# States scanned into SBUF, the last one kept by ScalarE, decays in four PSUM banks two steps ahead, four product buffers

## The chip, the core and the metric

The program runs on one core of a Trainium2 chip. The metric is the device time of one execution in microseconds (us). The core's engines run side by side and meet at semaphores: TensorE (PE, with its weight loads PEld) for matrix products, VectorE (DVE), ScalarE (ACT) and GpSimd (POOL) for elementwise work, SyncE (SP) for most transfers. SBUF is the working memory of 128 partitions, PSUM holds what TensorE writes, in 8 banks of 512 f32 elements a partition. GpSimd works on SBUF here.

## What is computed

4096 tokens (2 sequences of 2048) of width 256 pass through a mixture of experts with half weight, a Mamba block with an MLP behind it, and the same mixture of experts again. The change lies in the middle part. Cut to what matters, for each of 512 inner channels e and 16 states s:

```python
dA = jnp.exp(dt_t[..., None] * A)                       # decay
h = h * dA + (dt_t * u_t)[..., None] * B_t[:, None, :]  # state, a recurrence over the tokens t
y = jnp.einsum('bes,bs->be', h, C_t)                    # sum over the 16 states
...
y = tm(ys) + x_conv * D
y = y * silu(z)
return jnp.einsum('bte,de->btd', y, out_proj_w)
```

Behind it: `x = x + mamba(...)`, an rms norm, `square(relu(fc))` and a projection back to 256.

## The kernel before, in words

The middle part (`mamba`) takes the tokens in 8 chunks of 512 (CT), which lie in the free dimension; the 512 inner channels are 4 groups of 128 partitions, taken as 2 pairs p. For a chunk k (a "turn") there are 32 steps n = p*16 + s, one for each pair and state. A step does, for the two groups j of its pair:

- ScalarE, `decay`: dA = exp(A*DT) into PSUM bank B_DA + j (banks 2 and 3), one step ahead. It waits until the scan of the step before has read that bank (`scanned`).
- GpSimd, L1291: dB = DTU * B (one instruction of 128x1024, both operands in SBUF), into one of two buffers. It waits for the scans of two steps before, and so runs up to two steps ahead.
- VectorE, L1397: `tensor_tensor_scan`, h = dA*h + dB over 512 tokens, from PSUM (dA) and SBUF (dB) into PSUM bank B_H + j (banks 4 and 5). Its start value is a column of the state table ST.
- VectorE, L1406 (`weigh`): G = h * C, PSUM and SBUF in, SBUF out, two buffers; between the two weighs of a step L1413 copies the last column of both states into ST, with a bit mask that sets them to zero at the end of a sequence (`kept`).
- TensorE, L1101: transposes G and adds it into the sum over the states (banks 6 and 7).
- SP: loads the rows of B and C of the step, spread over the partitions, 4 buffers (L972).

Every engine runs its program in the order written. Besides the steps there is the work of the next chunk's front (norm, input product, convolution, dt) and of the chunk before's back (`out` product, norm, MLP). Tables (LATE, EARLY, BACK) say at which step n of a turn an engine does which item: the four numbers are the steps on PE, ACT, DVE and POOL. Those that matter here: on ScalarE `silu` at 19 (two table loads and two activations of 128x2048), `sq` at 9; on VectorE `out` at 5 and 7, `v` at 10 (L1378, the 128x4 sums of squares times 1/D plus eps), `pj` at 30 and 31; on GpSimd `add` (L1266, DT) at 6 and 27, `du` (L1270, DTU) at 7 and 28, `v` (L1276, the power -1/2) at 12, `xa` (L1280) at 14 and 16. Items stand behind the step's own work. At steps 0 and 16 VectorE does `gated` (L1365, 128x1024, PSUM and SBUF in) between the scans and the weighs.

In the mixture of experts two lines are spoken of below: L302 (VectorE, a product of two SBUF tensors of 320 elements) and L341 (GpSimd, a difference of two SBUF tensors of 320 elements), and L261, a short scan from SBUF to SBUF.

## Time and profile before

| | |
|---|---|
| time, median of 3 runs | 2183.04 us (2175.22 to 2190.57) |
| time of the profiled execution | 2182.28 us |
| its span (first to last instruction) | 2180.4 us |
| the scan stage in it | 591.8 to 1607 us |
| busy over the span | PE 1725.6, DVE 1709.5, POOL 1242.9, ACT 977.6 us |

The profile has one line for each instruction on each engine with its start and duration. A group of the costliest instructions is a line of the kernel with an engine and its shapes; behind it stand how often it ran, its busy time, its mean in ns, the idle time of the engine ahead of it and what ended that idle time ("<-DVE PS L1397" is: until VectorE's L1397 was done). In a timeline an instruction that has a release stands with it in square brackets. Instructions of one engine overlap by some tens of ns, so a chain of them is counted from start to start.

### The profile page before, as it was taken

The numbers are of one execution on the slowest core, as the hardware profiler recorded it, in microseconds if no ns is written. First come the engines' busy times: TensorE is split into PE (matmuls) and PEld (weight loads), VectorE is DVE, ScalarE is ACT, GpSimd is POOL, SyncE is SP. The second block draws the span as 40 slices with busy tenths as digits, with TensorE's granted clock in tenths as the row PEclk, the third lists the DMA queues.
The fourth block names the chain that finished last, engine by engine and source line by source line (L and its number), as shares of the span: only waits on it lengthen the run. The fifth ranks groups of instructions, "written<-read, shape, count | busy, mean of one in ns | idle before, by whom it ended". The sixth has DMA issues, their size and how long they took to land. (4 is left out here: it accounts for less than half of the span.)

```text
span 2180.4 us, 35658 instructions
## 1 busy us (share of the span) xinstructions
PE 1725.6 (79%) x10728; PEld 1411.5 (65%) x10729; DVE 1709.5 (78%) x2990; ACT 977.6 (45%) x1507; POOL 1242.9 (57%) x751
## 2 busy tenths in 40 slices
PE   5279999993886878879787787877577379999996
PEld 5279999993344546545464554545456269999996
DVE  4857666665498999989999999989955757766665
ACT  2333333331465566566666656665431323333331
POOL 1257455555476767767676676767631246545555
PEclk8589999997877898989999898988686579999998
DMA  6244343343343434434344443443412334333342
GB/s 193 79 120 105 69 86 82 82 70 90 121 137 126 140 127 141 136 122 143 127 136 127 137 136 127 136 128 136 142 36 97 97 102 106 81 74 87 82 78 26
DMA packets 161018, 237.96 MB, mean 109 GB/s; under 512 B 29370, under 2 KB 85296, under 8 KB 160304
## 3 DMA queue, kind: packets, MB, share of 16 engines
q1 hardware_dynamic: 130096, 198.84, 28.7%
q0 software_dynamic: 30720, 36.53, 10.1%
q8 instruction: 115, 1.88, 0.4%
q14 instruction: 87, 0.71, 0.1%
HBM read 202.57 MB, written 38.34 MB: 110 GB/s over the span
## 5 line engine op out<-in xcount | busy, mean ns | idle before, releaser
L1291 POOL TENSOR_TENSOR m_dB<-m_DTU,m_BC 128x1024 f32<-128x1024 f32 x256 | 604.0, 2362 | 308.0 <-DVE PS L1397 307.5
L1397 DVE TENSOR_TENSOR_SCAN PS<-PS,m_ST,m_dB 128x512 f32<-128x512 f32 x512 | 628.3, 1271 | 58.7 <-POOL m_dB L1291 27.1
L1110 ACT ACTIVATE PS<-m_DT,m_A 128x512 f32<-128x512 f32 x512 | 351.1, 690 | 361.3 <-DVE PS L1397 360.1
L1101 PEld LDWEIGHTS PS<-keep_ident,m_G 128*128 128x128 f32 x2048 | 254.9, 153 | 207.8 <-DVE m_G L1406 168.2
L1101 PE MATMUL PS<-keep_ident,m_G 128*128 128x128 f32 x2048 | 313.5, 297 | 90.2 <-DVE m_G L1406 89.7
L1406 DVE TENSOR_TENSOR m_G<-PS,m_BC 128x512 f32<-128x512 f32 x512 | 340.8, 673 | 10.3 <-PE PS L1101 10.2
L603 PE MATMUL PS<-e_xh,e_wh 128*128 128x256 f32 x1008 | 295.0, 293 | 0.5 <-DVEq L491 0.2
L603 PE MATMUL PS<-e_xl,e_wh 128*128 128x256 f32 x1008 | 289.0, 287 | 0.0
L603 PE MATMUL PS<-e_xh,e_wl 128*128 128x256 f32 x1008 | 288.8, 287 | 0.0
L660 ACT ACTIVATE e_hh<-e_u 128x512 fp32r<-128x512 f32 x252 | 157.9, 633 | 281.1 <-DVE e_u L716 280.9
L621 PE MATMUL PS<-e_wh,e_hh 128*128 128x256 f32 x1008 | 281.4, 279 | 0.0
L621 PE MATMUL PS<-e_wl,e_hh 128*128 128x256 f32 x1008 | 280.5, 278 | 0.0
L621 PE MATMUL PS<-e_wh,e_hl 128*128 128x256 f32 x1008 | 280.1, 278 | 0.0
L528 POOL DMA_INDIRECT e_xin<-xrows,e_gix x160 | 199.8, 1249 | 57.5 <-issue 43.1
L534 POOL DMA_INDIRECT out<-e_ysb,e_six x80 | 134.5, 1682 | 157.4 <-DVE e_ysb L740 136.7
L534 POOL DMA_INDIRECT sums<-e_ysb,e_six x80 | 136.8, 1710 | 150.4 <-DVE e_ysb L740 133.1
L735 DVE TENSOR_TENSOR e_ysb<-PS,e_b 128x512 f32<-128x512 f32 x80 | 55.2, 690 | 189.6 <-PE PS L621 184.0
L603 PEld LDWEIGHTS PS<-e_xh,e_wh 128*128 128x128 f32 x1008 | 198.6, 197 | 1.2 <-DVEq L491 0.8
L603 PEld LDWEIGHTS PS<-e_xl,e_wh 128*128 128x128 f32 x1008 | 198.8, 197 | 0.0
L603 PEld LDWEIGHTS PS<-e_xh,e_wl 128*128 128x128 f32 x1008 | 197.6, 196 | 0.0
L716 DVE TENSOR_TENSOR e_u<-PS,keep_b 128x512 f32<-128x512 f32 x252 | 170.0, 687 | 27.0 <-PE PS L603 16.1
L621 PEld LDWEIGHTS PS<-e_wl,e_hh 128*128 128x128 f32 x1008 | 189.3, 188 | 0.0
(200 smaller groups left out, 2908.1 us busy)
## 6 DMA issues: line engine op xcount, KB each, us to landing
m_BC<-bc_rows SPq DMA_DIRECT2D x512, 256.0 KB, 3.3
layer_raw<-w SPq DMA_DIRECT2D x64, 512.0 KB, 3.9
xrows<-r_xn SPq DMA_DIRECT2D x16, 512.0 KB, 4.2
keep_X<-x SPq DMA_DIRECT2D x4, 1024.0 KB, 9.6
sums<-keep_X SPq DMA_DIRECT2D x4, 1024.0 KB, 11.1
out<-keep_X SPq DMA_DIRECT2D x4, 1024.0 KB, 11.0
keep_X<-sums SPq DMA_DIRECT2D x3, 1024.0 KB, 13.4
e_xin<-xrows,e_gix POOLq DMA_INDIRECT x160, 3.3
```

What stands on the lines that cost most here:

```text
L528: G.indirect_dma_start(out=xin[:, c % CPE, t, :], out_offset=None, in_=xrows, in_offset=column(gix, c, t), bounds_check=last_token, oob_is ...
L534: G.indirect_dma_start(out=sums, out_offset=column(six, c, t), in_=ysb[:, c % CPE, t, :], in_offset=None, compute_op=ALU.add, bounds_check ...
L603: last = M(PS[:, B_S1 + pair, m * CH:(m + 1) * CH], a, r, start=(n == 0), stop=(n == len(terms) - 1))
L621: last = M(PS[:, B_Y + c % 2, t * D:(t + 1) * D], a, r, start=(n == 0), stop=(n == len(terms) - 1))
L660: A(hh[:, c % 2, 2 * pair:2 * pair + 2, :], u[:, pair, :, :], ACT.Relu).then_inc(hh_ok, 1)
L716: V.tensor_tensor(u[:, pair, :, :], PS[:, B_S1 + pair, :].rearrange("p (m c) -> p m c", m=2), b1.unsqueeze(2).to_broadcast([P, 2, CH]), AL ...
L735: V.tensor_tensor(ysb[:, c % CPE, :, :], PS[:, B_Y + c % 2, :].rearrange("p (t d) -> p t d", t=CHT), b2.unsqueeze(1).to_broadcast([P, CHT, ...
L1101: last = M(PS[:, B_Y + j, ts], G[:, s % 2, j, ts], C["ident"][:, :], is_transpose=True, start=False, stop=(s == DS - 1 and a == CTT - 1))
L1110: return nc.scalar.activation(out, in_, func, **kw)
L1291: G_.tensor_tensor(dB[:, s % 2, :, :], DTU[:, es, :], BC[:, s % NBC, 0:1, :].to_broadcast([P, 2, CT]), ALU.mult).then_inc(dB_ok, 1)
L1397: V.tensor_tensor_scan(PS[:, B_H + j, :], PS[:, B_DA + j, :], dB[:, s % 2, j, :], ST[:, s, e:e + 1], ALU.mult, ALU.add).then_inc(scanned, 1)
L1406: V.tensor_tensor(G[:, s % 2, j, :], PS[:, B_H + j, :], BC[:, s % NBC, 1, :], ALU.mult).then_inc(g_ok, 1)
```

## The change

- Scans write an SBUF buffer HS (two steps deep) and not PSUM; the weighs read it there.
- The two banks that the states had go to the decays: four banks, two steps ahead (`AHEAD`).
- G has four buffers in place of two.
- The last column of the states is copied into ST by ScalarE (`keep`: an ACTIVATE Copy with a scale of 1 or 0 from `fmask`), after the decays of the step, and VectorE's L1413 with its mask goes.
- `v`: ScalarE's Square takes the factor 1/sqrt(D); GpSimd adds eps just ahead of the power, and VectorE's L1378 goes. The item moves from GpSimd's step 12 to 11.
- To make room T3 and HID share one tensor TH of six parts, and hT is xrT.

The diff, without its imports and with the repeats of a pattern left out:

```diff
-        T3 = sb("T3", [P, EK, CT])
-        HID = sb("HID", [P, EK, CT])
+        TH = sb("TH", [P, 6, CT])
+        T3 = TH[:, 0:EK, :]
+        def hid(e, n=1):
+            at = e + 4 if e < 2 else e
+            return TH[:, at:at + n, :]
-        hT = sb("hT", [P, DK, CT])
+        hT = xrT
-        G = sb("G", [P, 2, 2, CT])
+        NG, NH = 4, 2
+        G = sb("G", [P, NG, 2, CT])
+        HS = sb("HS", [P, NH, 2, CT])
-        B_DA, B_H, B_Y = 2, 4, 6
+        B_DA, B_Y, AHEAD = 2, 6, 2
...
-("v", 0): (_, _, 10, 12),
+("v", 0): (_, _, _, 11),
...
@@ TensorE
-                                last = M(PS[:, B_Y + j, ts], G[:, s % 2, j, ts], C["ident"][:, :], is_transpose=True,
+                                last = M(PS[:, B_Y + j, ts], G[:, n % NG, j, ts], C["ident"][:, :], is_transpose=True,
@@ ScalarE
-                        last = F(XR[:, t, :], XP[:, t, :], ACT.Square, accum_out=ssq[:, t:t + 1])
+                        last = F(XR[:, t, :], XP[:, t, :], ACT.Square, scale=1.0 / math.isqrt(D), accum_out=ssq[:, t:t + 1])
...
-                    if not (is_first(k) and n == 0):
-                        act.wait_ge(scanned, k * (2 * STEPS) + (2 * (n - 1) + j + 1))
-                    F(PS[:, B_DA + j, :], DT[:, e, :], ACT.Exp, scale=A[:, e, s:s + 1]).then_inc(dA_ok, 1)
+                    if not (is_first(k) and n < AHEAD):
+                        act.wait_ge(scanned, k * (2 * STEPS) + (2 * (n - AHEAD) + j + 1))
+                    F(PS[:, B_DA + 2 * (n % AHEAD) + j, :], DT[:, e, :], ACT.Exp, scale=A[:, e, s:s + 1]).then_inc(dA_ok, 1)
+            def keep(k, p, s):
+                n = p * DS + s
+                F(ST[:, s, 2 * p:2 * p + 2], HS[:, n % NH, :, CT - 1], ACT.Copy, scale=fmask[:, bass.ds(k + 1, 1)]).then_inc(kept, 1)
...
-                        if n + 1 < STEPS:
-                            decay(k, (n + 1) // DS, (n + 1) % DS)
+                        if n + AHEAD < STEPS:
+                            decay(k, (n + AHEAD) // DS, (n + AHEAD) % DS)
                         elif has_front:
-                            decay(k + 1, 0, 0)
+                            decay(k + 1, 0, n + AHEAD - STEPS)
+                        if n + AHEAD < STEPS or has_front:
+                            keep(k, p, s)
@@ GpSimd
                 if kind == "v":
+                    gp.wait_ge(sq_ok, k + 1)
+                    G_.tensor_tensor(ssq[:, :], ssq[:, :], eps[:, :], ALU.add).then_inc(v_ok, 1)
                     gp.wait_ge(v_ok, k + 1)
                     G_.tensor_tensor(ssq[:, :], ssq[:, :], mhalf[:, 0, 0:CTT], ALU.pow).then_inc(rs_ok, 1)
@@ VectorE
-                elif kind == "v":
-                    dve.wait_ge(sq_ok, k + 1)
-                    V.tensor_scalar(ssq[:, :], ssq[:, :], 1.0 / D, RMS_EPS, ALU.mult, ALU.add).then_inc(v_ok, 1)
...
-                            if not (is_first(k) and n == 0):
-                                dve.wait_ge(g_ok, k * (2 * STEPS) + (2 * n + j - 1))
-                                dve.wait_ge(kept, k * STEPS + n)
+                            if not (is_first(k) and n < NH):
+                                dve.wait_ge(g_ok, k * (2 * STEPS) + (2 * (n - NH) + j + 1))
+                                dve.wait_ge(kept, k * STEPS + (n - NH + 1))
...
-                            V.tensor_tensor_scan(PS[:, B_H + j, :], PS[:, B_DA + j, :], dB[:, s % 2, j, :], ST[:, s, e:e + 1],
+                            V.tensor_tensor_scan(HS[:, n % NH, j, :], PS[:, B_DA + 2 * (n % AHEAD) + j, :], dB[:, s % 2, j, :], ST[:, s, e:e + 1],
...
-                            V.tensor_tensor(G[:, s % 2, j, :], PS[:, B_H + j, :], BC[:, s % NBC, 1, :], ALU.mult).then_inc(g_ok, 1)
+                            V.tensor_tensor(G[:, n % NG, j, :], HS[:, n % NH, j, :], BC[:, s % NBC, 1, :], ALU.mult).then_inc(g_ok, 1)
...
-                        if not (is_first(k) and n < 2):
-                            dve.wait_ge(g_read, k * STEPS + (n - 1))
+                        if not (is_first(k) and n < NG):
+                            dve.wait_ge(g_read, k * STEPS + (n - NG + 1))
                         weigh(0)
-                        dve.wait_ge(scanned, k * (2 * STEPS) + (2 * n + 2))
-                        V.tensor_tensor(ST[:, s, 2 * p:2 * p + 2].bitcast(U32), PS[:, B_H:B_H + 2, CT - 1].bitcast(U32),
-                                        mask[:, bass.ds(k + 1, 1)].to_broadcast([P, 2]), ALU.bitwise_and).then_inc(kept, 1)
                         weigh(1)
```

## Rows read from the trace of the kernel before

**Rows 1.** The page's first part: busy us (share of the span) xinstructions.

```profile
PE 1725.6 (79%) x10728; PEld 1411.5 (65%) x10729; DVE 1709.5 (78%) x2990; ACT 977.6 (45%) x1507; POOL 1242.9 (57%) x751
```

**Rows 2.** Windows: the scan stage; length, busy (x) of PE, PEld, DVE, ACT, POOL.

```profile
591.80:1607.00 1015.20, 800.11 (x3634) 528.72 (x3635) 970.68 (x1329) 621.46 (x973) 694.58 (x306) 0.87 0.41 132
```

**Rows 3.** Groups of the scan stage, shapes kept apart: busy, mean ns, idle before.

```profile
L1397 DVE TENSOR_TENSOR_SCAN PS<-PS,m_ST,m_dB 128x512 f32<-128x512 f32 x512 | 628.3, 1271 | 58.7 <-POOL m_dB L1291 27.1 <-ACT PS L1110 26.6 <-issue 4.2
L1406 DVE TENSOR_TENSOR m_G<-PS,m_BC 128x512 f32<-128x512 f32 x512 | 340.8, 673 | 10.3 <-PE PS L1101 10.2
L1413 DVE TENSOR_TENSOR m_ST<-PS,m_mask 128x2 uint32<-128x2 uint32 x256 | 36.3, 142 | 0.0
...
L1270 POOL TENSOR_TENSOR m_DTU<-m_DT,m_U 128x1024 f32<-128x1024 f32 x15 | 35.4, 2360 | 0.0
L1266 POOL TENSOR_TENSOR m_DT<-m_DT,m_sp 128x1024 f32<-128x1024 f32 x15 | 35.4, 2358 | 5.8 <-ACT m_sp L1110 5.8
L1280 POOL TENSOR_TENSOR keep_X<-keep_X,m_XP 128x512 f32 x12 | 15.3, 1277 | 0.0
L1276 POOL TENSOR_TENSOR m_ssq<-m_ssq,m_mhalf 128x4 f32<-128x4 f32 x7 | 7.1, 1018 | 0.7
```

**Rows 4.** Timeline: start, duration us; VectorE through steps 18 to 21, POOL once.

```profile
1047.85 2.45 DVE L1397 TENSOR_TENSOR_SCAN PS<-PS,m_ST,m_dB 128x512 f32<-128x512 f32 x2
1050.21 0.66 DVE L1406 TENSOR_TENSOR m_G<-PS,m_BC 128x512 f32<-128x512 f32 x1
1050.81 0.14 DVE L1413 TENSOR_TENSOR m_ST<-PS,m_mask 128x2 uint32<-128x2 uint32 x1
1050.87 0.67 DVE L1406 TENSOR_TENSOR m_G<-PS,m_BC 128x512 f32<-128x512 f32 x1
1051.47 2.45 DVE L1397 TENSOR_TENSOR_SCAN PS<-PS,m_ST,m_dB 128x512 f32<-128x512 f32 x2
...
1058.74 2.47 DVE L1397 TENSOR_TENSOR_SCAN PS<-PS,m_ST,m_dB 128x512 f32<-128x512 f32 x2 [3.58 <-ACT PS L1110]
...
1050.38 2.36 POOL L1291 TENSOR_TENSOR m_dB<-m_DTU,m_BC 128x1024 f32<-128x1024 f32 x1 [1.25 <-DVE PS L1397]
```

**Rows 5.** Timeline, ScalarE: decays around the silu block, and a small scaled copy.

```profile
1050.33 0.69 ACT L1110 ACTIVATE PS<-m_DT,m_A 128x512 f32<-128x512 f32 x1 [0.48 <-DVE PS L1397]
...
1057.93 1.30 ACT L1110 ACTIVATE PS<-m_DT,m_A 128x512 f32<-128x512 f32 x2
...
1001.47 0.29 ACT L1110 ACTIVATE m_XI<-m_XI,m_fmask 128x12 f32<-128x12 f32 x1
```

**Rows 6.** Line L1378 (ns min/median/max), and the timeline around one of them.

```profile
L1378 DVE TENSOR_SCALAR m_ssq<-m_ssq x8: 170/1305/1362, 760.7 to 1623.1; 128x4 f32<-128x4 f32 x8
...
1015.48 2.36 POOL L1291 TENSOR_TENSOR m_dB<-m_DTU,m_BC 128x1024 f32<-128x1024 f32 x1 [1.25 <-DVE PS L1397]
...
1016.57 1.30 DVE L1378 TENSOR_SCALAR m_ssq<-m_ssq 128x4 f32<-128x4 f32 x1
1017.78 2.46 DVE L1397 TENSOR_TENSOR_SCAN PS<-PS,m_ST,m_dB 128x512 f32<-128x512 f32 x2
```

**Rows 7.** First experts layer: timeline of L302 and L341, and the line L341.

```profile
86.62 0.88 DVE L302 TENSOR_TENSOR r_inblock<-r_hot,r_tile_no 128x320 bf16<-128x320 f32 x2
86.89 1.19 POOL L341 TENSOR_TENSOR r_hot<-r_count,r_high 128x320 f32<-128x320 f32 x1 [2.34 <-PE PS L409]
...
87.03 0.48 DVE L302 TENSOR_TENSOR r_inblock<-r_hot,r_tile_no 128x320 bf16<-128x320 f32 x1
...
L341 POOL TENSOR_TENSOR r_hot<-r_count,r_high x32: 713/721/1203, 79.1 to 1737.0; 128x320 f32<-128x320 f32 x32
```

**Rows 8.** Timeline of a step 16: gated on VectorE, dB on POOL.

```profile
1038.23 1.20 DVE L1365 TENSOR_TENSOR m_YT<-PS,m_SZ 128x1024 f32<-128x1024 f32 x1
...
1038.40 2.36 POOL L1291 TENSOR_TENSOR m_dB<-m_DTU,m_BC 128x1024 f32<-128x1024 f32 x1 [1.26 <-DVE PS L1397]
```

**Rows 9.** Timeline: the scans from SBUF to SBUF, 32 elements each.

```profile
69.10 2.10 DVE L261 TENSOR_TENSOR_SCAN r_inc<-r_zcol,r_tot 128x32 f32<-128x32 f32 x16
```

More of the change, by code:

```diff
@@ L1 @@
+import math
 import concourse.bass as bass
@@ L782, in mamba @@
         taps = sb("taps", [P, EK, DC, P])
-        mask = sb("mask", [P, MCH + 1], U32)
-        fmask = sb("fmask", [P, MCH])
+        fmask = sb("fmask", [P, MCH + 1])
         st = sb("st", [P, 2 * CTT, 6])
@@ L789, in mamba @@
         mhalf = sb("mhalf", [P, 2, 2 * CTT])
+        eps = sb("eps", [P, CTT])
         XI = sb("XI", [P, EK, DC - 1 + CT])
         U = sb("U", [P, 2, EK, CT])
-        T3 = sb("T3", [P, EK, CT])
-        HID = sb("HID", [P, EK, CT])
+        TH = sb("TH", [P, 6, CT])
[3 more added lines that the diff above has]
+            return TH[:, at:at + n, :]
         xrT = sb("xrT", [P, DK, CT])
-        hT = sb("hT", [P, DK, CT])
+        hT = xrT
         XR = sb("XR", [P, CTT, D])
@@ L848, in mamba @@
             ("g", 2): (1, 2, _, _), ("g", 3): (2, 3, _, _),
-            ("out", 0): (4, _, 5, _), ("out", 1): (6, _, 7, _), ("sq", 0): (_, 9, _, _), ("v", 0): (_, _, 10, 12),
+            ("out", 0): (4, _, 5, _), ("out", 1): (6, _, 7, _), ("sq", 0): (_, 9, _, _), ("v", 0): (_, _, _, 11),
             ("hr", 0): (_, 13, _, _), ("hT", 0): (19, 20, _, _), ("hT", 1): (21, 22, _, _), ("xa", 0): (_, _, _, 14), ("xa", 1): (_, _, _, 16),
@@ L1061, in back @@
                 elif kind in ("out", "pj"):
-                    at, src = (W_OUT, T3) if kind == "out" else (W_PJ, HID)
+                    at, src = (W_OUT, lambda e: T3[:, e:e + 1, :]) if kind == "out" else (W_PJ, hid)
                     if kind == "out":
@@ L1069, in back @@
                         for e in range(EK):
-                            last = M(bank(p, k)[:, (t % 2) * D:(t % 2 + 1) * D], src[:, e, t * P:(t + 1) * P],
+                            last = M(bank(p, k)[:, (t % 2) * D:(t % 2 + 1) * D], src(e)[:, 0, t * P:(t + 1) * P],
                                      weights(at, D, e, 0, D), start=(e == 0), stop=(e == EK - 1))
@@ L1208, in back @@
                     wait_written(act, p, k)
-                    F(HID[:, n, :], bank(p, k), ACT.Relu).then_inc(read(p, k), 1)
+                    F(hid(n)[:, 0, :], bank(p, k), ACT.Relu).then_inc(read(p, k), 1)
                 elif kind == "q":
                     wait_read(act, k, ("fc", 2 * n), ("fc", 2 * n + 1))
-                    F(HID[:, 2 * n:2 * n + 2, :], HID[:, 2 * n:2 * n + 2, :], ACT.Square).then_inc(q_ok, 1)
+                    F(hid(2 * n, 2), hid(2 * n, 2), ACT.Square).then_inc(q_ok, 1)
             def decay(k, p, s):
@@ L1222, in decay @@
                     e, n = 2 * p + j, p * DS + s
-                    if not (is_first(k) and n == 0):
-                        act.wait_ge(scanned, k * (2 * STEPS) + (2 * (n - 1) + j + 1))
-                    F(PS[:, B_DA + j, :], DT[:, e, :], ACT.Exp, scale=A[:, e, s:s + 1]).then_inc(dA_ok, 1)
+                    if not (is_first(k) and n < AHEAD):
[4 more added lines that the diff above has]
+                F(ST[:, s, 2 * p:2 * p + 2], HS[:, n % NH, :, CT - 1], ACT.Copy, scale=fmask[:, bass.ds(k + 1, 1)]).then_inc(kept, 1)
             def turn(k, par, has_front, has_back):
                 if is_first(k):
-                    decay(k, 0, 0)
+                    for s in range(AHEAD):
+                        decay(k, 0, s)
                 for p in range(PAIRS):
@@ L1301, in _ @@
             V.memset(mhalf[:, :, :], -0.5)
-            V.memset(fmask[:, :], 1.0)
-            link(V.memset(mask[:, :].bitcast(mybir.dt.int32), -1))
+            V.memset(eps[:, :], RMS_EPS)
+            link(V.memset(fmask[:, :], 1.0))
             V.memset(ST[:, :, :], 0.0)
@@ L1306, in _ @@
             for k in range(0, MCH, MCH // BATCH):
-                V.memset(fmask[:, k:k + 1], 0.0)
-                link(V.memset(mask[:, k:k + 1].bitcast(mybir.dt.int32), 0))
+                link(V.memset(fmask[:, k:k + 1], 0.0))
             def tile(k, t, n=1):
```

## The prediction

> **What bounds the kernel now.** I read the totals first [rows 1]. Over the whole span VectorE (DVE) and TensorE are both near 79% busy, which is an average over three stages. The diff touches one of them, the scan stage, so I cut it out: from the first scan at 591.8 us to 1607 us it lasts 1015 us, VectorE is busy for 971 of them, GpSimd (POOL) for 695 and ScalarE for 621 [rows 2]. VectorE sets the time there. Then the groups of that stretch [rows 3]: 512 scans, 512 products ("weigh", L1406) and 256 tiny state copies (L1413) make nearly all of VectorE's work. Its waits inside the stretch are small: 26.6 us for ScalarE's decays ahead of scans and 10.3 us for TensorE ahead of products; the 27.1 us put down to POOL are the wait before the very first scan.
>
> Next the timeline of one plain step [rows 4]: weigh at 1050.21, state copy at 1050.81, weigh at 1050.87, scans from 1051.47. Neighbours overlap a little, so I count start to start: 0.60 + 0.06 + 0.60 and 2.36 for the two scans, 3.62 us for a step. 256 steps of 3.62 are 927 us. POOL makes the next-but-one dB in 2.36 us of each step, starting 0.17 us after the first weigh, and sleeps 1.25 us. So POOL has slack today, and its work runs *at the same time* as the two weighs. That is legal today at no cost, because a weigh reads one operand from PSUM and one from SBUF. After the change it reads both from SBUF, and that is where my forecast turns.
>
> **The gains, part by part.**
>
> (a) State copy off VectorE: 0.06 to 0.07 us a step by the starts [rows 4], 256 steps: 17 us. The 142 ns of its row [rows 3] are mostly overlap. Its work goes to ScalarE; the nearest row is a small ACTIVATE with a pointer scale, 0.29 us [rows 5]. 256 of these are 75 us of an engine that idles for some 390 of 1015 us [rows 2]; it lies behind the decays and is needed only two steps later, so I cost it at nothing except in (c).
>
> (b) The tensor_scalar of L1378 leaves VectorE. It takes 170 ns with POOL idle and 1305 otherwise [rows 6]: seven times inside the stretch the next scan begins 1.21 us after it. 8.5 us.
>
> (c) Decays two steps ahead. At step 19 ScalarE runs a copy, two table loads and two silus between the decay at 1050.33 and the next at 1057.93 [rows 5], and VectorE stands 3.58 us [rows 4]. Afterwards scan 22 is the first to lack its decay. It is due three pairs of weighs and two pairs of scans after scan 19, 8.3 us by today's scans and 8.05 by those of (e). ScalarE is 0.7 us in the last decay, 0.3 in the copy, 6.9 in the block, then 1.25 in two decays and 0.25 in the copy that the scan now waits for: 9.3. About 1.2 us stay of 3.6. Seven turns and a shorter wait of the first chunk: 18 us gained. What is queued behind is then late by the keep as well: VectorE's scan waits for keep of two steps before, which stands in front of the block, so no new wait.
>
> (d) Four product buffers: weighs no longer wait for the transposes, 10 us of 10.3 [rows 3].
>
> (e) Scans write SBUF. No scan of 512 into SBUF is in the trace. Two points: start to start 1.18 for 512 into PSUM [rows 4], and 16 SBUF scans of 32 elements in 2.10 us [rows 9], so (2.10-0.21)/15 = 0.126. If the price is only elements, the slope is 2.2 ns and nothing is gained. If the fixed part is that of the other VectorE operations, about 0.06 us beside 1.04 ns an element (0.60 for 512 [rows 4], 0.40 for 320 [rows 7]), the short scan gives 2.1 ns an element, a long one 1.12, and the 0.06 left over belong to PSUM as destination. The bounds are 0 and 31 us; the common fixed part fits the more rows, so I take 31. A loss I exclude: VectorE already writes G to SBUF beside POOL at full rate [rows 4].
>
> (f) Weigh from two SBUF operands: 0 to +0.015 us each, I take +5 us in all. The weigh from PSUM (0.60 for 512) and the all-SBUF product (0.40 for 320) lie on one line of 1 ns an element.
>
> Sum of gains: 17 + 8.5 + 18 + 10 + 31 - 5 = 80 us. Buffers shared by T3/HID and xrT/hT cost nothing: their readers are done half a chunk before the next writer.
>
> The Trainium skill, VectorE: DVE Perf Modes, section on the TRN2 errata, gives 58 cycles beside the elements for SBUF to SBUF and 120 for PSUM to SBUF. It would shorten each weigh by 65 ns, 33 us in all; the line through the weigh and the all-SBUF product speaks against it.
>
> **The price: a door that both engines use.** L302 on VectorE multiplies two SBUF tensors, L341 on POOL reads two. A POOL L341 that starts 0.27 us into a pair of L302 takes 1.19 us in place of 0.72 (median 721, four such cases near 1200) and ends 0.72 after 87.37, that is when the *second* L302 has read its input [rows 7]. So POOL stands while VectorE reads two SBUF operands, and it isn't let in between two such products that follow closely. The other way round, L1378 ran until POOL's dB was over: end 1017.87 beside 1017.84 [rows 6]; the engine that waits gets in about 0.15 us before the recorded end of the other. That is a one-source operation; whether a two-source one is held likewise no row shows. I take it that it is.
>
> The Trainium skill, SBUF — State Buffer, section Who interferes with whom, says so: a Vector instruction with two SBUF inputs contends with a GpSimd instruction that reads SBUF, and who comes second is held for the whole instruction. For L341 the trace agrees (1194 to 1203 ns beside 721).
>
> Now a plain step after, with 0 at the first weigh: weighs at 0 and 0.60, door free at 1.13, dB runs 1.13 to 3.49, VectorE could enter from 3.35. Scans start at 1.20 and 2.32, next weigh at 3.43 (3.55 if (e) fails). It just fits: a plain step costs nothing. But POOL's slack is gone, and dB is only two buffers deep, so nothing is caught up. Every other visit to the door lands on VectorE:
> - `add` and `du`, 2.36 us each [rows 3], 30 in the stretch (two a chunk of either, less the two made before it). They begin as dB ends, hold the door to 5.80, the weigh enters at 5.65: 2.1 us each, 63. (If the weigh comes first by a hair, the next dB is late and the scan waits 2.3 instead.) Seven of them lie behind a VectorE `out`, 0.6 less each: 59.
> - `xa`, 1.27 us: 14 times 1.0, 14 us. `v`: its add of eps and the pow of 1.02 us, which waits behind the weighs and pushes dB: 7 times 0.8, 6 us.
> - At `gated` (steps 0 and 16) VectorE does a product from PSUM for 1.12 us first [rows 8], POOL's dB takes the door 0.17 us in and keeps it to 2.4: 1.25 us, 15 times, 19 us.
>
> Price 98 us. Net +18. The sum is made on the profiled execution (span 2180.4, time 2182.3, 0.8 below the median of the three runs); 2183 + 18.5 = 2202.
>
> **Rivals.**
> 1. The door is contended, but scans gain nothing from SBUF (e = 0; (c) gains 2 more): 2202 + 31 - 2 = 2231. For it: one slope of 2.2 also fits. 0.22.
> 2. The door costs nothing for f32 products beside dB, because a two-source read is not held by a running POOL instruction and dB isn't pushed past its due time. Then only gains are left: 2183 - 80 = 2103, or 2133 without (e). Its place is the weigh at 3.43; it decides from the point where add, du, xa and gated cost under 2.6 us a chunk in place of 12. For it: no row shows a held two-source product. Against it: L341. 0.13. A half-way form, in which only POOL is held and the 1.2 us between dB's end and the scan that needs it hide part of each visit (30 x 1.2 and the 19 of gated): 2202 - 55 = 2147, 0.06.
> 3. Weighs from SBUF also lose 0.06 us each: 2202 - 31 = 2171. Only the page on VectorE speaks for it (it says 65 ns). 0.08.
> 4. POOL gets in between the two weighs of a step. Then the second begins at 2.75, a step lasts 5.7 in place of 3.43: 256 x 2.27 = 581 more, less the 98, 2685. Against it: L302's pair held together with POOL waiting since 0.27; for it: there is a semaphore wait between the weighs. 0.06.
> 5. ScalarE's extra copies or anything else: 0.03.
>
> **How the numbers follow.** My forecast has 0.42, about 2188 to 2216. A measurement here can tell about 1% from no change, 22 us: 2161 to 2205. Rival 2 and its half-way form lie below: 0.20 with a little of 5. Rival 3 and somewhat over half of the forecast lie within: 0.35. The rest of the forecast, rivals 1 and 4 lie above: 0.45. For 8 in 10 the range must hold the forecast, 1, 3 and the half-way form, and a margin: 2125 to 2245.
>
> **What the profile after would show.** Right: weighs of some 0.68 us in plain steps and a second form of about 2.8 us (once for each add and du) or 1.9 (gated); dB of 2.36 in place but recorded as some 3.3 us, since it starts as before and waits; POOL busy near 900 us in the stretch; no idle before weighs by TensorE; ScalarE's wait near 1.2 us a chunk; scan starts 1.12 apart. Wrong: dB stays at 2.36 with weighs running beside it (rival 2); scans still 1.18 apart (rival 1); every second weigh near 2.9 (rival 4). A plain step longer than 3.6 us would say that the fit of dB between the weighs fails, and that I mis-sized the handing over of the door.

## The result, and the profile after

The changed kernel takes **2643.62 us** (median of 4 runs, 2641.18 to 2647.44) beside 2184.43 for the kernel before (4 runs on the same chip). The ratio is 1.2118, 95% interval 1.2088 to 1.2148. The forecast was 2202 with a range of 2125 to 2245; the time lies nearest to rival 4 (2685), which had a chance of 0.06.

The page's first part and the windows of the scan stage, after (columns as in [rows 1, 2]):

```profile
PE 1870.9 (71%) x10726; PEld 1472.0 (56%) x10729; DVE 2215.3 (84%) x2724; ACT 1032.2 (39%) x1761; POOL 1339.9 (51%) x759
...
591.40:2068.00 1476.60, 947.64 (x3634) 592.17 (x3634) 1476.55 (x1065) 674.87 (x1225) 793.43 (x313) 0.78 0.28 91
```

The whole loss lies in the stage that the change touches. It lasted 1015 us [rows 2] and lasts 1477; outside it both executions spend 1165 us. VectorE has 264 instructions fewer there and is busy for all of it, 1476.55 of 1476.60 us. The granted TensorE clock fell with TensorE's share of the time (0.87 to 0.78 in the stage), but no wait of VectorE for TensorE is left, so it sets nothing.

The groups of the stage, after (line, engine, operation, tiles, shapes, count; busy, mean ns; idle before), and then what the line of the weighs says (ns minimum, median, maximum):

```profile
L1423 DVE TENSOR_TENSOR m_G<-m_HS,m_BC 128x512 f32<-128x512 f32 x511 | 856.8, 1714 | 0.0
L1414 DVE TENSOR_TENSOR_SCAN m_HS<-PS,m_ST,m_dB 128x512 f32<-128x512 f32 x512 | 626.0, 1261 | 26.1 <-POOL m_dB L1312 26.1
...
L1312 POOL TENSOR_TENSOR m_dB<-m_DTU,m_BC 128x1024 f32<-128x1024 f32 x255 | 681.5, 2672 | 669.5 <-DVE m_HS L1414 669.5
L1289 POOL TENSOR_TENSOR m_DTU<-m_DT,m_U 128x1024 f32<-128x1024 f32 x15 | 42.0, 2797 | 0.0
...
L1121 ACT ACTIVATE m_ST<-m_HS,m_fmask 128x2 f32<-128x2 f32 x254 | 71.4, 281 | 0.0
...
L1423 DVE TENSOR_TENSOR m_G<-m_HS,m_BC x512: 655/679/2855, 593.8 to 2068.0; 128x512 f32<-128x512 f32 x171
```

Scans are what they were (1261 ns beside 1271 in [rows 3]). The weighs went from a mean of 673 to 1714 ns, but not evenly: the median is 679, the maximum 2855. That is two kinds, one weigh untouched and one very long. VectorE's idle time is nothing except the wait before the first scan. A kernel that has lost 460 us shows *no waits* on the engine that sets its time: the loss stands inside the duration of an instruction, and only the gap between median and mean gives it away.

The timeline of one step, after (start, duration us; VectorE, then GpSimd):

```profile
1171.06 3.42 DVE L1423 TENSOR_TENSOR m_G<-m_HS,m_BC 128x512 f32<-128x512 f32 x2
1174.40 2.44 DVE L1414 TENSOR_TENSOR_SCAN m_HS<-PS,m_ST,m_dB 128x512 f32<-128x512 f32 x2
...
1171.21 2.72 POOL L1312 TENSOR_TENSOR m_dB<-m_DTU,m_BC 128x1024 f32<-128x1024 f32 x1 [2.99 <-DVE m_HS L1414]
1174.19 2.50 POOL L1285 TENSOR_TENSOR m_DT<-m_DT,m_sp 128x1024 f32<-128x1024 f32 x1 [0.26 <-ACT m_sp L1121]
1176.93 2.71 POOL L1312 TENSOR_TENSOR m_dB<-m_DTU,m_BC 128x1024 f32<-128x1024 f32 x1 [0.23 <-DVE m_HS L1414]
```

The first weigh begins at 1171.06. GpSimd's dB starts at 1171.21 and is recorded as 2.72 us in place of 2.36, so it stands about 0.4 us, as long as that first weigh reads. The second weigh starts at 1171.64 and lasts 2.84 us, to 1174.48. If it needs its usual 0.66 once it is let in, it was let in at 1173.8, 0.11 us before dB's recorded end at 1173.93. The step is 5.71 us from scan to scan where it was 3.62 [rows 4]. GpSimd's `add` at 1174.19 stands for the last 0.14 us of that weigh (2.50 in place of 2.36), then runs beside the scans and costs VectorE nothing: the slack that the forecast saw disappear has come back, because the step is now so long.

**The sum closes.** From the first to the last step's scans lie 255 steps: 1011.9 us before, 1473.6 after, 461.7 more. Plain steps: 255 x 2.09 (5.71 less 3.62) = 533. A turn of 32 steps had 11.3 us beyond 32 plain steps before (127.1 less 115.8: `gated`, `out`, `pj`, `v`, and the waits for decays and transposes) and has 2.9 after (185.6 less 182.7): `gated` adds 0.24 in place of 1.13, as dB runs meanwhile, and the waits are gone. 8.4 x 8 = 67 less, which leaves 466.

### The profile page after: what moved, and what is told of

Read it like the earlier page. It is cut to its first block and busy times, and to the rows that moved or that the text cites. A ratio compares the mean times of both kernels' runs of the same rounds, so it can differ in the third digit from the quotient of the medians.

```text
span 2641.6 us, 35668 instructions
## 1 busy us (share of the span) xinstructions
PE 1870.9 (71%) x10726; PEld 1472.0 (56%) x10729; DVE 2215.3 (84%) x2724; ACT 1032.2 (39%) x1761; POOL 1339.9 (51%) x759
## 5 line engine op out<-in xcount | busy, mean ns | idle before, releaser
L1312 POOL TENSOR_TENSOR m_dB<-m_DTU,m_BC 128x1024 f32<-128x1024 f32 x256 | 683.8, 2671 | 669.5 <-DVE m_HS L1414 669.5
L1423 DVE TENSOR_TENSOR m_G<-m_HS,m_BC 128x512 f32<-128x512 f32 x512 | 857.4, 1712 | 0.0
L1112 PE MATMUL PS<-keep_ident,m_G 128*128 128x128 f32 x2048 | 391.8, 330 | 412.2 <-DVE m_G L1423 411.1
L1414 DVE TENSOR_TENSOR_SCAN m_HS<-PS,m_ST,m_dB 128x512 f32<-128x512 f32 x512 | 626.0, 1261 | 26.1 <-POOL m_dB L1312 26.1
L1112 PEld LDWEIGHTS PS<-keep_ident,m_G 128*128 128x128 f32 x2048 | 279.2, 167 | 588.3 <-DVE m_G L1423 550.4
L737 DVE TENSOR_TENSOR e_ysb<-PS,e_b 128x512 f32<-128x512 f32 x80 | 55.2, 690 | 187.4 <-PE PS L623 182.7
```

The source lines that it names most:

```text
L737: V.tensor_tensor(ysb[:, c % CPE, :, :], PS[:, B_Y + c % 2, :].rearrange("p (t d) -> p t d", t=CHT), b2.unsqueeze(1).to_broadcast([P, CHT, ...
L1112: last = M(PS[:, B_Y + j, ts], G[:, n % NG, j, ts], C["ident"][:, :], is_transpose=True, start=False, stop=(s == DS - 1 and a == CTT - 1))
L1312: G_.tensor_tensor(dB[:, s % 2, :, :], DTU[:, es, :], BC[:, s % NBC, 0:1, :].to_broadcast([P, 2, CT]), ALU.mult).then_inc(dB_ok, 1)
L1414: V.tensor_tensor_scan(HS[:, n % NH, j, :], PS[:, B_DA + 2 * (n % AHEAD) + j, :], dB[:, s % 2, j, :], ST[:, s, e:e + 1], ALU.mult, ALU.add ...
L1423: V.tensor_tensor(G[:, n % NG, j, :], HS[:, n % NH, j, :], BC[:, s % NBC, 1, :], ALU.mult).then_inc(g_ok, 1)
```

## The experiments

Two causes were conceivable at once for a second weigh of 2.84 us: the door (the prediction's word for what VectorE and GpSimd can't use together while both read two SBUF operands) or the scans' new place; and within the door, why GpSimd gets in between two weighs that are 0.58 us apart, start to start. Times without a range are single runs.

### 1. GpSimd asks after both weighs, and after the first

dB's own wait is for the scans of two steps before; here it waits for the weighs of that step, so that no dB can ask while one is under way.

```diff
-                            gp.wait_ge(scanned, k * (2 * STEPS) + (2 * n - 2))
+                            gp.wait_ge(g_ok, k * (2 * STEPS) + (2 * n - 2))   # e1; e2: 2 * n - 3
```

> The changed kernel, with one edit: GpSimd's dB of step n waits until both weighs of step n-2 are done (g_ok) in place of the scans of step n-2, so it asks for SBUF only while VectorE scans. Theory A (GpSimd's read gets in between the two weighs of a step and holds the second for 2.2 us): steps of 3.55 to 3.65 us in place of 5.71, both weighs near 0.66 us, dB at 2.36 us; add, du, xa and gated now cost their 10 to 13 us a chunk, so about 2644 - 256 x 2.1 + 98 = 2205 to 2250 us in all. Theory B (two-source products are slow beside any GpSimd work, whatever the order): steps stay over 5 us, total above 2550.

> As e1, but dB of step n waits for the first of the two weighs of step n-2 only, so that it asks about 0.1 us after the second weigh has begun. Theory A (what matters is who asks first): the second weigh is not held, dB is recorded 0.3 to 0.5 us longer than 2.36, step 3.55 to 3.7, total within 10 us of e1. If GpSimd is favoured whenever it waits, the second weigh is still near 2.8 us and the total near 2640.

Measured: e1 **2231.31 us** (2230.1 to 2233.29), 1.0223 of before (1.0201 to 1.0244), so 412 us of the 460 are back by an edit of one wait. e2: 2218.41, 13 below e1 where 10 had been allowed. Timeline of e1 around an `add`, VectorE, then GpSimd; last, e2's pair and its dB:

```profile
1014.21 1.30 DVE L1423 TENSOR_TENSOR m_G<-m_HS,m_BC 128x512 f32<-128x512 f32 x2
1015.44 2.44 DVE L1414 TENSOR_TENSOR_SCAN m_HS<-PS,m_ST,m_dB 128x512 f32<-128x512 f32 x2
1017.81 3.46 DVE L1423 TENSOR_TENSOR m_G<-m_HS,m_BC 128x512 f32<-128x512 f32 x2
...
1015.59 2.37 POOL L1312 TENSOR_TENSOR m_dB<-m_DTU,m_BC 128x1024 f32<-128x1024 f32 x1 [1.23 <-DVE m_G L1423]
1017.92 2.80 POOL L1285 TENSOR_TENSOR m_DT<-m_DT,m_sp 128x1024 f32<-128x1024 f32 x1
```

```profile
1008.52 1.27 DVE L1423 TENSOR_TENSOR m_G<-m_HS,m_BC 128x512 f32<-128x512 f32 x2
...
1009.27 2.76 POOL L1312 TENSOR_TENSOR m_dB<-m_DTU,m_BC 128x1024 f32<-128x1024 f32 x1 [0.81 <-DVE m_G L1423]
```

In e1 a plain pair of weighs takes 1.30 us and dB 2.37 beside the scans, in time: the plain step is 3.58. The pair at 1017.81 met an `add` that started 0.11 us later, and is 3.46 long: the second weigh is held, the price of the door that the forecast had put on `add` and `du`. In e2 dB starts 0.16 us after the *second* weigh, is itself held (2.76) and the weigh isn't. So whoever comes second to an instruction under way waits, and in the changed kernel the next product of VectorE then comes after him: in all 239 steps in which a dB starts between the starts of the two weighs, the second is held. This is the cause of the loss; the scans' place has no part in it, since e1 keeps it.

### 2. One SBUF operand less

The second operand of a weigh is the next step's decay, in PSUM.

```diff
+                            other = BC[:, s % NBC, 1, :]
+                            if n + 1 < STEPS or has_front:
+                                dve.wait_ge(dA_ok, k * (2 * STEPS) + (2 * n + j + 3))
+                                other = PS[:, B_DA + 2 * ((n + 1) % AHEAD) + j, :]
```

> The changed kernel, but the weigh multiplies the state in SBUF by the next step's decay in PSUM and not by the row of C in SBUF (the sum over the states is then another one; everything else runs as it did). It has one SBUF operand left. Theory A (the cause is the second SBUF operand): weighs at 0.66 to 0.68, no wait on GpSimd, step 3.55, dB 2.36, and the gains alone are seen: 2183 - 50 = 2125 to 2140 us. Theory B (the cause is the state written to and read from SBUF, whatever the other operand): still 5 us a step and more, over 2500 us.

Measured: **2149.77 us**, 32 below the kernel before on that chip and 10 above the expected range. The pair, its dB and the group of the weighs:

```profile
985.41 1.27 DVE L1427 TENSOR_TENSOR m_G<-m_HS,PS 128x512 f32<-128x512 f32 x2
...
985.58 2.37 POOL L1312 TENSOR_TENSOR m_dB<-m_DTU,m_BC 128x1024 f32<-128x1024 f32 x1 [1.18 <-DVE m_HS L1414]
...
L1427 DVE TENSOR_TENSOR m_G<-m_HS,PS 128x512 f32<-128x512 f32 x510 | 324.1, 681 | 18.6 <-ACT PS L1121 18.6
```

GpSimd starts dB 0.17 us into the pair, as in the kernel before, and neither is held. One operand in PSUM opens the door completely. The 18.6 us that VectorE waits for a decay come from this edit's own wait; without them it would, by estimate, be near 2131. So the whole change without its door would be worth some 50 us (2181.34, the time before on that chip, less 2131), also an estimate.

### 3. States in SBUF, and nothing else

The kernel before, with scans into HS and weighs and state copy from there.

```diff
+        HS = sb("HS", [P, 2, 2, CT])
-                            V.tensor_tensor_scan(PS[:, B_H + j, :], PS[:, B_DA + j, :], ...
+                            V.tensor_tensor_scan(HS[:, s % 2, j, :], PS[:, B_DA + j, :], ...
```

> The kernel before with one part of the change alone: scans write the states to SBUF, and the weighs and VectorE's small state copy read them there; decays one step ahead, two G buffers, the tensor_scalar on VectorE, all as before (T3 and HID share room, hT is xrT). If the place of the states is the whole cause, GpSimd's dB gets in behind the first weigh: steps of 5.7 to 5.8 and 2640 to 2700 us in all, the small copy or the second weigh held for 2.2 us. If the loss needs another part of the change: under 2300.

Measured: 2659.11 us, so this part alone carries the loss. Here the state copy stands between the weighs, and it is what is held:

```profile
L1418 DVE TENSOR_TENSOR m_ST<-m_HS,m_mask x256: 147/2301/2326, 593.7 to 2086.7; 128x2 uint32<-128x2 uint32 x128
```

Two elements a partition take 2.3 us, and the second weigh behind it 0.68. It is the place in the order that decides, not the size of the instruction.

### 4. Why does GpSimd get in between the two weighs?

The forecast had held it shut out, since L341 was shut out between two L302 [rows 7]. Four differences were tried. **The time of asking**: ahead of dB come 3, 5 or 7 small memsets (behind a semaphore increment), so that it starts later after the first weigh.

```diff
+                        gp.sem_inc(asked, 1)
+                        G_.memset(st[:, ...], 0.0)          # 3, 5 or 7 of them
                         G_.tensor_tensor(dB[:, s % 2, :, :], DTU[:, es, :], BC[...], ALU.mult)
```

> The changed kernel; on GpSimd, ahead of every dB, a semaphore increment and three memsets of 6 to 12 columns in a tensor that nobody reads any more, which put dB's start from 0.16 to about 0.5 us after the first weigh's start, a little before the second's at 0.58. In the experts' layer a GpSimd instruction that began 0.14 us before the second of two such products was not let in between. If the time of asking decides, the second weigh is no longer held: 0.68 us, steps near 3.6, total 2210 to 2270. If what lets GpSimd in is something else between the weighs (the semaphore wait, the longer product), the second weigh is still held, near 2.8 us, steps of 5.7 to 6.0, total 2640 to 2720.

> As e4, with five memsets of 3 columns ahead of dB. In e4 three of them put dB's start at 0.36 us after the first weigh's, 0.22 before the second's, and the second was still held. Five should put it at 0.44, 0.14 before the second, where the experts' layer has its four cases that were not let in (0.136 to 0.145 before). Theory C (the time of asking decides, and GpSimd asks for SBUF some 0.15 to 0.2 us after its recorded start): the second weigh goes at once in most steps, steps 3.6 to 3.8, total 2210 to 2280; the edge may be mixed. Theory D (two products that follow closely are parted whenever GpSimd has begun before the second): held, steps 5.7, total near 2650.

> As e8 with seven memsets: dB starts at about 0.52, 0.06 before the second weigh. Theory C: second weigh at 0.68 us in all plain steps, dB recorded near 3.0, total 2200 to 2260. Theory D: held, 2650.

Measured: 2651.7, 2631.09 and 2615.2 us; dB mostly starts 0.22, 0.17 and 0.11 us before the second weigh (0.43 in the changed kernel). A step of the last of them, VectorE's pair and GpSimd:

```profile
1160.50 0.66 DVE L1432 TENSOR_TENSOR m_G<-m_HS,m_BC 128x512 f32<-128x512 f32 x1
1161.08 2.84 DVE L1432 TENSOR_TENSOR m_G<-m_HS,m_BC 128x512 f32<-128x512 f32 x1
...
1160.97 2.40 POOL L1321 TENSOR_TENSOR m_dB<-m_DTU,m_BC 128x1024 f32<-128x1024 f32 x1
```

Even a dB that starts while the first weigh is nearly over mostly comes first and holds the second: of 159 steps of e9 with dB 0.11 us ahead, 154 have a held second weigh (median 2833 ns). So a long wait isn't what earns the turn. Only in 3 steps with dB 0.02 us ahead is the second weigh always 0.68 us long, while one dB that starts 0.06 us ahead in the changed kernel does hold it (2.86 us). In 16 steps of e9 dB starts 0.14 to 0.19 us after the second weigh, and holds nothing.

But a start before the second weigh isn't enough either. In six steps of e9 (0.11 to 0.12 us ahead) and three of e8 (0.17 to 0.18) the pair stays together and dB waits for both weighs, 3.0 to 3.1 us. One of them, VectorE, then GpSimd:

```profile
908.25 1.26 DVE L1432 TENSOR_TENSOR m_G<-m_HS,m_BC 128x512 f32<-128x512 f32 x2
...
908.73 3.01 POOL L1321 TENSOR_TENSOR m_dB<-m_DTU,m_BC 128x1024 f32<-128x1024 f32 x1
```

The instructions and the distance are those of the 154. All nine lie where GpSimd's large instruction before had ended less than 0.7 us before the first weigh; so had it in 71 steps of these two runs in which the second weigh was held. What tells the two outcomes apart isn't shown. The times of e8 and e9 are below the 2650 expected of a held weigh because in 14 and 25 of their steps the second weigh isn't held. (Three memsets were to put dB's start 0.5 us after the first weigh's and put it at 0.36: they start 0.03 to 0.04 us apart. A form with one memset of 128x300 in their place had no room in SBUF, so it has no time.)

**The wait and the signal between the weighs**: e5 takes both waits for scans ahead of the first weigh, e12 takes the increment off the first weigh, e11 does both. In e5 and e11, and in e6 and e15 below, GpSimd also has an increment and one small memset ahead of dB, so that VectorE starts first.

```diff
-                            dve.wait_ge(scanned, k * (2 * STEPS) + (2 * n + j + 1))    # in weigh(j): e5, e11
+                        dve.wait_ge(scanned, k * (2 * STEPS) + (2 * n + 2))            # ahead of both
-                            V.tensor_tensor(G[...], HS[...], BC[...], ALU.mult).then_inc(g_ok, 1)   # e11, e12
+                            last = V.tensor_tensor(G[...], HS[...], BC[...], ALU.mult)
+                            if j == 1:
+                                last.then_inc(g_ok, 2)
```

> The changed kernel with both waits for the scans in front of the first weigh, so that none stands between the two; and on GpSimd a semaphore increment and one small memset ahead of dB, so that VectorE stays the first to ask. If the wait between the weighs is what lets GpSimd in, the second weigh is not held: steps near 3.7, total 2230 to 2290. If GpSimd gets in wherever one instruction ends and the next has not yet asked, the second weigh is still held: 2.7 to 2.8 us, steps near 5.8, total 2640 to 2700.

> As e5 (no wait between the weighs, GpSimd's dB behind a semaphore increment and one memset), and the first weigh raises no semaphore any more; the second raises it by two. Then the pair stands as the two products of the experts' layer do that were not parted: no wait, no signal between. Theory E (the signal at the end of the first product, or the wait, makes VectorE let go of the second read port): second weigh 0.68 us, steps 3.6 to 3.8, total 2220 to 2280. Theory F (any gap between two such products lets a waiting GpSimd in, and the experts' case differs by something else): second weigh 2.8 us, steps 5.9, total near 2700 as e5.

> The changed kernel with one edit: the first weigh raises no semaphore, the second raises it by two; the wait for the second scan stays between them. If e11 is not held, this tells signal from wait: not held here (total 2200 to 2260) would put it on the signal alone, held (second weigh 2.8 us, 2640 to 2660) on the wait or on both. If e11 is held, this is held too.

Measured: 2701.59, 2699.26 and 2640.16 us. With neither (e11: `x512: 676/694/2861` on the weighs' line) the second is held as before, 2833 ns. The bare pair of e5:

```profile
1194.99 0.69 DVE L1425 TENSOR_TENSOR m_G<-m_HS,m_BC 128x512 f32<-128x512 f32 x1
1195.60 2.85 DVE L1425 TENSOR_TENSOR m_G<-m_HS,m_BC 128x512 f32<-128x512 f32 x1
...
1195.08 2.83 POOL L1315 TENSOR_TENSOR m_dB<-m_DTU,m_BC 128x1024 f32<-128x1024 f32 x1
```

Rival 4's only argument had been the semaphore wait between the weighs. It isn't the reason. (e5 and e11 are 56 to 58 us slower than the changed kernel because the first weigh also waits for the second scan's end.)

**The operands' pattern**: L302 reads an operand that is repeated. e13 repeats one column of C for the weighs, e14 one column of B for dB.

```diff
-... BC[:, s % NBC, 1, :], ALU.mult)
+... BC[:, s % NBC, 1, 0:1].to_broadcast([P, CT]), ALU.mult)                # e13, weigh
-... BC[:, s % NBC, 0:1, :].to_broadcast([P, 2, CT]),
+... BC[:, s % NBC, 0:1, 0:1].to_broadcast([P, 2, CT]),                    # e14, dB
```

> The changed kernel, but the weigh's second operand is one column of C repeated 512 times (step 0 in the access pattern) and not the row of C; the sum over the states is then another one. In the experts' layer L302's second operand is such a repeated column. Theory G (VectorE keeps the port over two products, or does not need it, when the second operand is a repeated column): second weigh 0.68 us, steps 3.55 to 3.8, total 2130 (port not used at all, dB 2.36) to 2260 (dB near 3.3). Theory F2 (the operand's pattern plays no part): second weigh 2.8 us, total 2640.

> The changed kernel, but GpSimd's dB reads one column of B repeated, as L341 in the experts' layer reads a repeated column (the states are then others). If it is GpSimd's pattern that kept it out of the pair there, the second weigh is not held: total 2200 to 2260, or dB is shorter as well (2.0 in place of 2.36, by L341's 0.72 for 320 elements against 0.86 by dB's rate). If not, second weigh held for dB's time: 2.5 to 2.8 us, total 2550 to 2640.

Measured: 2649.42 and 2525.71 us. The weighs' line of e13, and those of the weighs and of dB in e14:

```profile
L1423 DVE TENSOR_TENSOR m_G<-m_HS,m_BC x512: 657/679/2855, 594.5 to 2068.9; 128x512 f32<-128x512 f32 x171
```

```profile
L1423 DVE TENSOR_TENSOR m_G<-m_HS,m_BC x512: 657/784/2389, 589.6 to 1950.0; 128x512 f32<-128x512 f32 x171
...
L1312 POOL TENSOR_TENSOR m_dB<-m_DTU,m_BC x256: 1894/2256/2347, 585.2 to 1940.2; 128x1024 f32<-128x1024 f32 x128
```

For VectorE a repeated column is as good as a full operand. For GpSimd it shortens dB to 1.9 us, and the held weigh follows: 2.38 in place of 2.83. The weigh is held for as long as dB itself takes, which e14 shows by changing only that. (2525.71 is 24 below what had been expected of a held weigh, since dB was taken to be 2.0 us long at best.)

**The length**: L302 has 320 elements. e15 cuts each weigh into 320 and 192 columns.

```diff
+                            V.tensor_tensor(G[:, n % NG, j, 0:320], HS[:, n % NH, j, 0:320], BC[:, s % NBC, 1, 0:320], ALU.mult)
+                            V.tensor_tensor(G[:, n % NG, j, 320:], HS[:, n % NH, j, 320:], BC[:, s % NBC, 1, 320:], ALU.mult).then_inc(g_ok, 1)
```

> The changed kernel, each weigh as two products of 320 and 192 columns with nothing between them, and dB behind a semaphore increment and one memset, so that dB starts about 0.28 us after the first product and 0.12 us before the second. Length and times are then those of the pair of L302 and L341 in the experts' layer; the output type (f32 here, bf16 there) and the work in front are not. Theory H (length and times decide): the second product (192) is not held; the gap ahead of the second weigh is passed in the same way or lets dB in there: steps 3.8 or 5.9, and the 192-column product at 0.33 us. Theory I (they don't): the 192-column product is held, 2.5 us, steps near 5.9, total 2680 to 2720.

Measured: 2749.26 us. Both pieces of a first weigh, and dB:

```profile
1201.54 0.46 DVE L1426 TENSOR_TENSOR m_G<-m_HS,m_BC 128x320 f32<-128x320 f32 x1
1201.92 2.50 DVE L1427 TENSOR_TENSOR m_G<-m_HS,m_BC 128x192 f32<-128x192 f32 x1
...
1201.83 2.37 POOL L1315 TENSOR_TENSOR m_dB<-m_DTU,m_BC 128x1024 f32<-128x1024 f32 x1
```

The pieces start 0.38 us apart, closer than the pair in [rows 7], and GpSimd, 0.09 us ahead of the second, comes in between. (The time is above the expected 2720: where `add`, `du` or `xa` run as well, two pieces of a step are held.)

Here too it isn't always so. In five steps dB starts within 0.01 us of the second piece and is let in at neither of the two changes from piece to piece that follow:

```profile
684.80 0.35 DVE L1427 TENSOR_TENSOR m_G<-m_HS,m_BC 128x192 f32<-128x192 f32 x1
685.07 0.48 DVE L1426 TENSOR_TENSOR m_G<-m_HS,m_BC 128x320 f32<-128x320 f32 x1
685.47 0.35 DVE L1427 TENSOR_TENSOR m_G<-m_HS,m_BC 128x192 f32<-128x192 f32 x1
...
684.81 3.24 POOL L1315 TENSOR_TENSOR m_dB<-m_DTU,m_BC 128x1024 f32<-128x1024 f32 x1
```

dB stands for 0.88 us (3.24 less 2.36), to 0.2 us into the last piece. This is what L341 did between two L302, in the same kernel and with f32 output.

### 5. One instruction in place of two

If the turn can pass only between instructions, a weigh that is one instruction can't be parted. The wait for both scans stands ahead of it, as in e5.

```diff
+                        V.tensor_tensor(G[:, n % NG, :, :], HS[:, n % NH, :, :], BC[:, s % NBC, 1:2, :].to_broadcast([P, 2, CT]),
+                                        ALU.mult).then_inc(g_ok, 2)
```

> As e5, but the two weighs are one instruction of 128x1024. If GpSimd gets in only between instructions, nothing is held after VectorE has begun: weigh of 1.2 us, dB recorded at about 3.3 us, steps near 3.6 to 3.7, total 2220 to 2280 us, like the run in which dB waits for the weighs. If GpSimd's dB still takes its turn first, the weigh takes 3.4 us and the total is near 2650.

```profile
1021.63 1.23 DVE L1428 TENSOR_TENSOR m_G<-m_HS,m_BC 128x1024 f32<-128x1024 f32 x1
1022.77 2.45 DVE L1417 TENSOR_TENSOR_SCAN m_HS<-PS,m_ST,m_dB 128x512 f32<-128x512 f32 x2
...
1021.71 3.37 POOL L1315 TENSOR_TENSOR m_dB<-m_DTU,m_BC 128x1024 f32<-128x1024 f32 x1
```

Measured: 2254.51 us (2252.49 to 2258.06), 1.0305 of before (1.0274 to 1.0337). dB starts 0.08 us into the weigh, stands for all of it (3.37 less 2.36 is 1.0) and runs beside the scans. That is the picture the prediction had drawn for the changed kernel, dB of "some 3.3 us" among it, and here it took one instruction in place of two close ones.

### 6. The parts that keep off the door

The kernel before with two parts of the change: four product buffers, and `v` without VectorE (with the memory that these need). States stay in PSUM.

```diff
+        NG = 4
+        G = sb("G", [P, NG, 2, CT])
-("v", 0): (_, _, 10, 12),
+("v", 0): (_, _, _, 11),
```

> The kernel before with two parts of the change alone: four G buffers, and the eps of the sums of squares added on GpSimd (with the shared T3/HID for room). States stay in PSUM, so every weigh has one SBUF operand; VectorE keeps its small state copy; decays are one step ahead. Theory A: no weigh is held; gains are the 1.2 us of the held tensor_scalar seven times, 8.5 us, and of the 10.3 us that weighs waited for TensorE those that a deeper buffer can hide, 3 to 10 us: 2181 - 12 to 18 = 2163 to 2169 us, 0.6 to 0.9% under the kernel before. If nothing is gained: 2181.

Measured, 7 runs beside 12 of the kernel before: **2175.01 us** (2170.53 to 2176.99) and 2188.01, ratio **0.9941** (0.9920 to 0.9962). That is 0.6% less than the kernel before, clear of the interval but small. The groups of its scans and weighs:

```profile
L1405 DVE TENSOR_TENSOR_SCAN PS<-PS,m_ST,m_dB 128x512 f32<-128x512 f32 x512 | 628.9, 1273 | 65.2 <-ACT PS L1118 31.6 <-POOL m_dB L1301 29.0 <-issue 3.7
L1414 DVE TENSOR_TENSOR m_G<-PS,m_BC 128x512 f32<-128x512 f32 x512 | 341.2, 675 | 0.0
```

The 10.3 us ahead of weighs are gone, and about 7 of them come back ahead of scans (31.6 for ScalarE and 29.0 for GpSimd, 26.6 and 27.1 in [rows 3]), nearly all at step 23: without the one wait VectorE is earlier at the next one.

## Why the prediction was wrong, point by point

**Rival 4 happened.** The step that failed is the sentence "it isn't let in between two such products that follow closely". It rested on one place, L302 and L341, four cases in the whole trace, of another output type and another length, and it was carried to 256 steps whose cost depended on it: 2.1 us each, against 0 if it held. In the changed kernel dB is let in 239 times out of 239. Nor is the opposite a rule: e8, e9 and e15 have 14 steps in which GpSimd is kept out as L341 was, beside hundreds in which it isn't. [Rows 7] showed the *door*, and that part was right: e3 opens it with one operand in PSUM, e1 and e2 show either engine held. What they couldn't carry is who gets the turn. The forecast gave 0.06 to a rival of +500 us on the strength of a pattern seen in one place; with two candidate rules (turn by instruction, turn by closeness) and one unlike example, a quarter or more would, as I judge it now, have been fair, and the range should have said that it left this case out.

**Its size.** Rival 4's step of 5.7 is the 5.71 measured, its second weigh at 2.75 after the first with 0.6 to go is the 2.84 recorded from 0.58. Its 2685 was 41 us high: about 13 for `gated`, of whose 1.13 us in each of 15 steps 0.89 is now hidden, and 8 for the rest of ScalarE's wait, which a step of 5.7 us swallows. The other 20 aren't itemised.

**The other terms,** read from the kernels in which the weighs aren't parted. Distances from one step's scans to the next, medians over the six middle turns, in us:

| step | before | after | e1 | e3 |
|---|---|---|---|---|
| plain | 3.62 | 5.71 | 3.58 | 3.55 |
| 0, 16 (`gated`) | 4.75 | 5.95 | 4.68 | 4.68 |
| 5, 6 (`add`, `du`, an `out` at 5) | 4.21, 3.62 | 6.31, 5.71 | 6.35, 5.29 | 4.14, 3.55 |
| 10, 11 (`v`) | 4.84, 3.62 | 5.71, 5.70 | 3.60, 4.36 | 3.54, 3.55 |
| 13, 15 (`xa`) | 3.62, 3.62 | 5.71, 5.71 | 4.67, 4.66 | 3.54, 3.55 |
| 20 to 23 (behind the silus) | 19.6 | 22.8 | 17.2 | 17.0 |
| 26, 27 (`add`, `du`) | 3.62, 3.62 | 5.71, 5.71 | 5.76, 5.73 | 3.54, 3.55 |

- (a) The state copy off VectorE: right, 0.063 us from its start to the next weigh's, 16 us. With the weighs (f), 3.62 to 3.55 in e3 and e2, 17 us. In e1 only 3.58: the two weighs of its pairs start 0.614 us apart in place of 0.583, and the first has a median of 691 ns (666 in e2). Why isn't shown.
- (b) `v` off VectorE: right, 4.84 to 3.60 at step 10, 1.2 us seven times.
- (c) Decays two ahead: right. The first late scan behind the silus, that of step 22, waits 1.24 us in six of the seven turns of e1 (forecast 1.2), 8.3 in all, where the same block cost 24.8 before.
- (d) Four buffers: right as to the wait (0.0 ahead of the weighs), but mis-sized as a gain, nearly nothing in e1 in place of 10. Of the 10.3 us before, 9.6 stood at step 22 of the turns; in e1 9.5 come back ahead of the scans of step 24, and with the 8.3 they make the 17.8 us that its scans wait for ScalarE. That second wait isn't the silu block, which is over by then. ScalarE stands 4.33 us for TensorE (L1059) ahead of a copy, and the decays of step 24 are queued behind that copy (e1, ScalarE, then VectorE):

```profile
1093.20 0.59 ACT L1121 ACTIVATE m_XD<-PS 96x512 f32<-96x512 f32 x1 [4.33 <-PE PS L1059]
1093.69 1.29 ACT L1121 ACTIVATE PS<-m_DT,m_A 128x512 f32<-128x512 f32 x2
...
1095.48 2.46 DVE L1414 TENSOR_TENSOR_SCAN m_HS<-PS,m_ST,m_dB 128x512 f32<-128x512 f32 x2 [1.48 <-ACT m_ST L1121]
```

  VectorE waited for TensorE directly before, and does so through ScalarE now. The forecast followed neither queue beyond its first wait.
- (e) Scans into SBUF: failed, 0 of 31. Start to start 1.19 us for the first and 1.175 for the second scan of a step, before and after. The forecast had a choice of two readings of one short scan and took the one with the gain.
- (f) Weighs from SBUF: from start to start the first of a step is 8 ns shorter (0.591 to 0.583), the second, where it isn't held, 4 ns longer (0.598 to 0.602 in e1, e2 and e9). That is 1 us gained in place of 5 lost, and rival 3 is out. The Trainium skill, VectorE: DVE Perf Modes, section on the TRN2 errata, gives 58 and 120 cycles beside the elements, from which an estimate of 65 ns less for each weigh follows; the traces give 8 ns at most.
- The price of the door on other visits: e1 shows it almost as forecast. `add` and `du` 2.15 each (forecast 2.1; 1.7 for the `du` behind the first `add`), `xa` 1.05 to 1.1 (1.0), `v` 0.8 (0.8). `gated` costs nothing there, since dB waits for the weighs behind it. e1 came out at 2231, which was rival 1's number, and that is luck: `gated` costs nothing in e1 (19 less), (c) and (d) bring 19 in place of the 30 of rival 1 (11 more), and plain steps are 3.58 in place of 3.55 (8 more).

The Trainium skill, SBUF — State Buffer, section Who interferes with whom, says that the one who comes second is held for the whole instruction. The runs agree (2.84 in place of 0.66 us on VectorE, 2.76 in place of 2.36 on GpSimd).

**What stays open.** What decides, between two products of VectorE, whether a waiting GpSimd is let in. It always is in the changed kernel, and never in the four cases of L341. The wait, the signal, the repeated operand and the length don't decide it by themselves (e5, e11 to e15). The time of asking isn't ruled out: L341 starts 0.14 us ahead of the second L302, and at 0.11 to 0.18 us e8 and e9 show both outcomes, though 9 against more than 400. L302's bf16 output and what stands ahead of either instruction there weren't tried; the five steps of e15 show that an f32 pair can keep GpSimd out as well. Whether the turn passes at the end of an instruction's reads or by some other event between them isn't shown either.

## What to carry to other kernels

Before an operand of a VectorE product moves from PSUM to SBUF, look at what GpSimd does at that moment: if it reads SBUF too, each such pair costs up to GpSimd's whole instruction, on whichever engine comes second. Count two VectorE products in a row as two visits, however close they stand: the one place where they held together didn't foretell the rest. Make them one instruction (e6, 2254.51), keep one operand in PSUM (e3), or let GpSimd wait for the first (e2, 2218.41) or the last of them (e1, 2231.31). None of these made the whole change pay here, except e3, which computes something else. And in a profile without waits look for a group whose mean is far above its median: that is where such a loss is recorded.

## What was new about the hardware

- A GpSimd instruction that starts 0.11 us or more before the second of two VectorE products 0.58 us apart is nearly always served between them (239 of 239 in the changed kernel, all but 9 of over 400 in e8 and e9); at 0.02 us it isn't (3 of 3).
- The turn doesn't pass at every change of instruction: in five steps of e15 GpSimd waited through three VectorE products, 0.88 us.
- A held instruction of either engine, if it takes its usual time once let in, began 0.11 to 0.15 us before the recorded end of the other.
- A 128x2 operation is held as long as a 128x512 one: 2.30 us in e10.
- A repeated column as operand leaves VectorE's product at 0.68 us and shortens GpSimd's 128x1024 from 2.36 to 1.9 us.
- A scan of 512 elements takes 1.19 us from start to start whether it writes PSUM or SBUF.
